# An FFN step on TensorE: the next image's first product placed ahead of the second product of two images back

## The reference

```python
def bitlinear(x, w, g):
    xn = rmsnorm(x, g)
    xq = xn + stop_gradient(act_quant(xn) - xn)      # 8-bit steps, one scale for each row
    wq = w + stop_gradient(weight_quant(w) - w)      # -1, 0, 1 and one scale
    return einsum('bsd,fd->bsf', xq, wq)
h = h + bitlinear(gelu(bitlinear(layernorm(h), w1, g1)), w2, g2)    # 192 -> 768 -> 192
```

## Time and profile before

| | us |
|---|---|
| median of 3 runs | 1763.29 |
| lowest, highest | 1759.63, 1763.37 |
| profiled execution, its own time | 1756.74 |
| profiled execution, span | 1755.0 |
| first stage, up to the first FFN operation of DVE | 1227.30 |
| FFN stage | 527.7 |

### The profile page before, as it was taken

The page is one execution under the profiler, slowest core; times in us unless marked ns, Lnnn a source line. Parts: engine busy times, 40 slices in busy tenths (PEclk is TensorE's granted clock), DMA queues, the critical chain, the costliest instruction groups (busy, mean ns, idle before and its releaser), DMA issues.

```text
span 1755.0 us, 53767 instructions
## 1 busy us (share of the span) xinstructions
PE 1477.3 (84%) x18602; PEld 1206.3 (69%) x18602; DVE 1442.4 (82%) x3227; ACT 1238.5 (71%) x1862; POOL 1102.7 (63%) x1369
## 2 busy tenths in 40 slices
PE   5799999999999999999999999984556565656565
PEld 2678888888888888888888888873445454545454
DVE  5588888888888888888888888864899999999996
ACT  1476767667676777767677776752788888888887
POOL 5456565666666666666666666541777777777775
PEclk8799999999999999999999999996687778787776
DMA  8533334343433343434343434320000000000000
GB/s 211 79 56 66 62 61 66 60 67 60 67 60 68 59 68 57 70 56 71 53 74 53 74 54 72 56 56 18 9 24 20 24 20 24 20 24 20 24 20 29
DMA packets 104194, 93.57 MB, mean 53 GB/s; under 512 B 22737, under 2 KB 94466, under 8 KB 104162
## 3 DMA queue, kind: packets, MB, share of 16 engines
q1 hardware_dynamic: 103394, 91.58, 27.6%
q0 software_dynamic: 768, 1.57, 0.4%
HBM read 74.12 MB, written 11.91 MB: 49 GB/s over the span
## 4 chain that ended last, share of the span: by engine, by line
PE 64%; DVE 14%; issue 10%; ACT 5%; POOL 3%; DVEq 1%; DMA 1%; SPq 0%; ACTq 0%; POOLq 0%
PE ps L1038 18%; PE ps L1095 9%; PE ps L1181 8%; DVE ff_st L814 4%; PE ps L1172 4%; PE ps L1280 4%; PE ps L1128 3%; PE ps L1160 3%; PE ps L1154 3%; PE ps L1261 3%; ACT probs L881 3%; POOL probs L440 2%; PE ps L1086 2%; PE ps L1076 2%; PE ps L1133 2%
## 5 line engine op out<-in xcount | busy, mean ns | idle before, releaser
L1038 PE MATMUL ps<-w_eff,pix 124*112 124x193 f32 (+1 forms) x2048 | 408.2, 337 | 11.0 <-DMA pix<-side 7.6
L677 DVE TENSOR_REDUCE nmax<-ps 116x12 bf16<-116x1344 f32 (+2 forms) x192 | 302.2, 1574 | 96.7 <-PE ps L1133 95.1
L493 POOL TENSOR_TENSOR pix<-probs,g_b 112x192 f32<-112x192 f32 (+1 forms) x512 | 299.2, 615 | 103.6 <-ACT probs L993 94.3
L881 ACT ACTIVATE probs<-ps,isw 116x688 f32<-116x688 f32 x384 | 299.1, 831 | 83.7 <-PE ps L1160 82.9
L1038 PEld LDWEIGHTS ps<-w_eff,pix 124*112 124x112 f32 (+1 forms) x2048 | 309.1, 167 | 37.7 <-issue 22.5
L440 POOL TENSOR_SCALAR_AFFINE_SELECT probs<-probs 116x464 f32<-116x464 f32 x384 | 277.2, 734 | 65.5 <-ACT probs L881 57.2
L420 POOL TENSOR_TENSOR xsq<-xsq 124x784 f32<-124x784 f32 (+1 forms) x128 | 184.3, 1440 | 210.0 <-ACT xsq L874 205.0
L863 ACT ACTIVATE pix<-xpix 54x896 f32<-54x896 f32 (+1 forms) x128 | 196.1, 1534 | 0.8
L1250 PE MATMUL ps<-ident_h,xpix 112*96 112x112 f16 (+1 forms) x256 | 34.9, 281 | 185.1 <-DVE xpix L831 185.0
L1095 PE MATMUL ps<-xnT,wq_pad 97*128 97x228 f32 (+1 forms) x768 | 166.4, 366 | 0.0
L1250 PEld LDWEIGHTS ps<-ident_h,xpix 112*96 112x96 f16 (+1 forms) x256 | 23.8, 168 | 196.8 <-DVE xpix L831 99.1
(11 more groups left out here) (134 smaller groups left out, 3143.1 us busy)
## 6 DMA issues: line engine op xcount, KB each, us to landing
xpix<-in_x SPq DMA_DIRECT2D x192, 196.0 KB
rden<-den_rows SPq DMA_DIRECT2D x256, 85.5 KB, 2.2
out<-xpix SPq DMA_DIRECT2D x64, 87.0 KB
out<-xpix SPq DMA_DIRECT2D x64, 84.0 KB
xpix<-in_x SPq DMA_DIRECT2D x128, 34.1 KB
h_all<-shift_w SPq DMA_DIRECT2D x5, 768.0 KB, 4.5
pix<-side SPq DMA_DIRECT2D x64, 36.8 KB
pix<-side SPq DMA_DIRECT2D x64, 36.6 KB
```

What stands on the lines that cost most here:

```text
L493: last = nc.gpsimd.tensor_tensor(v2[0:P, b, tile, cols], gel[0:P, b, tile, cols], g2_b[0:P, cols], ALU.mult)
L677: V.tensor_reduce(dst, src, AX_X, ALU.max, negate=True).then_inc(s_mx, 1)
L881: A(probs[0:TB, g, 2 * e:2 * e + 2, :], ps[0:TB, 4 + 2 * e:6 + 2 * e, 0:SK], ACT.Exp, scale=isw[0:TB, 7:8]).then_inc(s_p, 1)
L1038: last = MM(ps_tok[tile][0:P, :], pix[0:HI, par, o, lo:lo + P], w_eff[0:HI, o, :], start=(o == 0), stop=(o == OFFS - 1))
```

## The change

In PE's `ffn_step`, `ffn_first(i + 1)` stands ahead of `ffn_second(i - 2)`. Nothing else differs: the same instructions with the same waits, on PE alone. The order of the other engines is untouched.

```diff
             def ffn_step(i, new=True, mid=True, last_=True):
                 if new:
                     turn_first(i + 1)
+                if new:
+                    ffn_first(i + 1)
                 if last_:
                     ffn_second(i - 2)
-                if new:
-                    ffn_first(i + 1)
                 if mid:
                     turn_second(i - 1)
```

## The result

The changed kernel takes 1897.63 us (median of 4 runs, 1897.20 to 1897.99); the kernel before takes 1762.51 us (4 runs, 1759.63 to 1763.37). The ratio is 1.0767, with a 95% interval of 1.0753 to 1.0781: slower by 7.7%. The profiled execution took 1897.99 us, its span is 1896.3 us.

A forecast was written before the change was run, and what follows sets the result against it. DVE's own work was taken to bound the FFN stage. A loop of 10.2 instead of 7.96 us over 60 steps adds 134.4, with the end 136: 1893 from the profiled 1756.74, 1900 by the median; predicted 1896, range 1845 to 1935.

The forecast's parts named there:

- DVE's work bounds the kernel before: FFN stage: DVE, 93% busy, sets the pace; it waits only 5.0 us in all for the second product.
- L807 is late: DVE's take-up of the second product comes late by 3.43 us at 1.2 GHz or 0.94 at 2.4, delaying everything behind.
- The terms: Step loop at low clock: 6.36 us from q1 to y plus a 4.01 us DVE tail, 10.37; 10.2 taken.
- The clock: PE idles about 2.9 us before each step, so each starts at 1.2 GHz; loop between 9.95 and 10.37 us.
- The short tail: DVE from L807 to q1's end: 4.01 us at 1.2 GHz, as POOL is just done when L820 starts at 8.94.
- the rival with the longer tail: Low clock, DVE's tail stays 4.65 us because POOL is later: loop 11.01, 1942 us; chance 0.10.
- DVE's busy share: DVE's busy share of the FFN stage falls from 93% to about 70%, with L831 and L821 shorter.
- The end: Step 62: the moved product stands behind the last turn_first; y late by up to 3.7 us, 2 counted.
- the clock stays high: PE stays at the high clock for most of the path: loop 8.93 to 9.7, 1817 to 1863 us; chance 0.10.
- nothing changes: Only DVE's load counts and PE's sum of work is the same: 1757 us; chance 0.04.
- the earlier gelu makes the kernel faster: POOL gets its rows up to 0.61 us earlier and each step shortens by this: 1720 us; chance 0.03.

The follow-up runs named there:

- b_y_late: Kernel before the change, with DVE's final rows y moved behind L814, L820 and L821: 1761.77 us.
- b_warm: Kernel before the change, with 24 matmuls whose result nobody reads added at the end of each PE step: 1737.82 us.
- a_second_last: Changed kernel, with the second product moved also behind turn_second on PE: 1967.21 us.
- a_y_late: Changed kernel, with DVE's final rows y moved behind L814, L820 and L821, ahead of the reciprocal: 1831.36 us.
- a_y_last: Changed kernel, with DVE's final rows y moved behind q1 to the step's end, reading a copy of their scales: 1832.73 us.
- a_three: Changed kernel, with y behind q1, turn_second ahead of the second product, and two buffers for q2T: 1742.38 us.
- a_split_first: Changed kernel, but only the first product's first tile stands ahead of the second product, its second tile behind: 1878.31 us.
- a_warm_40: Changed kernel, with 40 matmuls whose result nobody reads added at the end of each PE step: 1829.12 us.

## Why the prediction was right

The forecast was 1896 and the result 1897.63. Point by point:

- *DVE's work bounds the kernel before, and only 5 us of waiting lie at L807.* b_y_late shows the second half: taking that wait away changes nothing. The prediction held PE's speed to count for nothing beside it. b_warm shows that it does count, by 25 us, and its trace puts most of that on POOL and DVE's statistics.
- *L807 is late, and all behind it with it.* Shown by the 211.2 us of waiting in 60 of 60 steps, by the dose (a_second_last), by a_y_late and a_y_last, which took half of the loss away, and by a_three, in which the second product is in neither loop and the loss is gone.
- *The terms.* From q1 to y the sum was 6.36 us at 1.2 GHz and the trace has 6.24; for the tail 4.01 and 4.02; for the loop 10.2 was chosen, and it was 10.24 over 60 steps. The first hand-overs and the copy of q1T stand in the step above as in the sum. The second product took 1.81 us and not 2.17, and from its end to y it was 0.24 us (1509.13 to 1509.37) and not 0.04, which gives back part of that.
- *The clock.* Each step was to start at 1.2 GHz. The idle stretch ahead of turn_first became 3.7 us, where 2.9 was forecast (turn_second ran at 2.4 GHz and was done sooner), and no transpose of turn_first took under 297 ns, where some had taken 212 before. The clock rose only during the second product, so nearly the whole path ran low. The parts are those of the sum with the clock low, 10.37. That 10.2 came within 0.04 us of the measured loop is in part luck: it was picked between 9.95 and 10.37, and no row said where between them. One step in two stretches and the start of the next (columns as in the earlier trace rows):

```profile
1503.30:1508.40 5.10, 4.24 (x19) 3.26 (x20) 2.14 (x10) 3.98 (x6) 2.57 (x4) 0.50 0.00 0
1508.60:1512.40 3.80, 1.14 (x18) 0.97 (x16) 2.84 (x7) 2.63 (x5) 3.14 (x6) 0.95 0.13 40
1512.70:1518.60 5.90, 4.30 (x19) 3.31 (x20) 3.07 (x14) 4.09 (x7) 2.58 (x4) 0.50 0.00 0
```

- *The short tail.* Here the prediction read its own numbers too kindly, and luck helped. It had L820 start 8.94 us after q1's end and POOL end at about 9.0, so POOL was still at work by 0.06 us and not "just done". In the step above POOL's multiplications took 4.62 us and not 4.87, they end at 1511.89, and L820 starts at 1511.95, 0.06 us on the other side. So the short tail held (L821 takes 170 ns on average between 1300 and 1700 us, and 500 before), and the rival with the longer tail, 1942, did not come. a_split_first shows that tail, 4.65 us.
- *DVE's busy share.* About 70% was forecast and 60% came (367.52 of 614.31 us). The prediction took the meeting with POOL out of the tail only; L785 and L789, ahead of L807, are shorter too (169 ns each on average in the same stretch, where they took 462 and 283). This is not in the sum, as DVE waits at L807 in any case. It is one reason why that wait became 3.5 us and 211.2 in all, just above the 2 to 3.4 and the 120 to 200 forecast: in the step above DVE is ready for y 2.53 us after q1's end, and not 2.93.
- *The end.* 2 us were counted for step 62 and none came: from the last turn_first to the end it is 24.7 us, and 24.8 before. Of the 6.6 us between the profiled execution and the median I took half; some 4.5 us of them were a quick first stage in that one execution. So the match to 2 us in the total is closer than the working earns.
- *The rivals.* That the clock stays high did not come; a_warm_40 shows what it would have been, 1829, inside the 1817 to 1863 given for it. That nothing changes, and that the earlier gelu makes the kernel faster, both fell to the wait at L807.
- *What the prediction did not see.* It asked what is late on DVE, and not whether another loop lay just under the one it found. The loop of PE and ACT, 9.1 us, was hidden under 10.24: in the changed kernel ACT waits for turn_first ahead of its copy of q1T 83.9 us in 59 times, 1.4 us each, which leaves an estimated 8.8 for that loop. The earlier trace rows have 2.56 + 1.92 + 1.03 us of it on PE, and ACT's copy, squares and copy follow. The forecast did not need it, but those of a_y_late and a_y_last did.

## What to carry to other kernels

When a product moves on PE, ask which instruction of another engine takes it up, at which time of the step, and what stands behind that instruction: here PE, busy 61% of the time, came to set the pace of DVE, busy 93%. Sum the new loop from one engine's release back to itself, and then look for the next loop through the same product, because taking away the first wait pays only down to the second: 10.24 us came down to 9.1 here, and not to 7.9. A reorder that loses by itself can be part of a gain once its consumers are moved too: 1897.63 and 1742.38 us, both with the first product ahead of the second.

## What I had not expected of the hardware

Keeping TensorE at 2.4 GHz with matmuls that nobody reads made the kernel before 1.4% faster (0.9842 to 0.9875), though DVE and not TensorE bounds it. And a DVE operation on two columns (L785) takes 169 ns on average where it is clear of POOL's multiplications, as in b_warm, and 462 ns in the kernel before, where they often overlap, so it matters to DVE when POOL ends its work.
